# Cross-attention on one core: gamma steps, loads of the next batch and remainders of weights in another order

## What is computed

```python
a = layer_norm(ctx) * gamma + beta              # [512, 1024] of each batch
Q, K, V = x @ Wq.T, a @ Wk.T, a @ Wv.T          # 16 heads of 64
scores = where(mask, Q @ K.T * 64 ** -0.5, -inf)
out = softmax(scores) @ V                       # back to [512, 1024]
y = x + tanh(gate) * (out @ Wo.T)
```

## Time and profile before

| | us |
|---|---|
| median of 3 runs (1990.89 to 1993.92) | 1991.17 |
| profiled execution | 1995.22 |
| its span | 1993.4 |
| TensorE (PE) busy | 1941.4 (97%) |
| VectorE (DVE) busy | 1618.6 (81%) |
| GpSimd (POOL) busy | 1573.6 (79%) |
| ScalarE (ACT) busy | 1284.8 (64%) |
| DMA queue q1, share of 16 engines | 51.4% |

### The profile page before, as it was taken

How to read it: one execution, slowest core, us unless ns; L and a number is a source line. 1 busy time by engine, 2 the same in 40 slices (tenths; PEclk the granted TensorE clock), 3 DMA queues, 4 the chain that set the end, 5 groups by cost and what they waited for, 6 DMA issues and landing times.

```text
span 1993.4 us, 26143 instructions
## 1 busy us (share of the span) xinstructions
PE 1941.4 (97%) x8528; PEld 1570.1 (79%) x8528; DVE 1618.6 (81%) x2089; ACT 1284.8 (64%) x2375; POOL 1573.6 (79%) x851
## 2 busy tenths in 40 slices
PE   6999999999999999999999999999999999999997
PEld 5777778887788777888788887888778888788886
DVE  7688878887788777888788887888778888778878
ACT  5767776567656576655865668665686566756554
POOL 3899997789867888678876789768897688966664
PEclk9999999999999999999999999999999999999999
DMA  7577545664365543664446553555534655435422
GB/s 265 180 246 254 180 158 188 207 218 159 122 216 179 196 175 111 232 203 167 153 149 216 186 204 121 182 198 186 203 124 156 234 161 191 150 129 191 155 103 107
DMA packets 150039, 356.67 MB, mean 179 GB/s; under 512 B 63504, under 2 KB 67600, under 8 KB 149008
## 3 DMA queue, kind: packets, MB, share of 16 engines
q1 hardware_dynamic: 149904, 354.99, 51.4%
HBM read 303.54 MB, written 51.39 MB: 178 GB/s over the span
## 4 chain that ended last, share of the span: by engine, by line
PE 65%; ACT 8%; POOL 8%; DVE 7%; DMA 6%; issue 3%; SPq 2%; POOLq 0%; ACTq 0%; DVEq 0%
PE pj L485 12%; PE pj L487 12%; PE pj L489 12%; PE sc L438 4%; PE sc L442 4%; PE sc L439 4%; PE pv L432 4%; PE sc L412 4%; PE sc L413 4%; PE pv L433 4%; POOL a_lo L1189 4%; DVE mq L847 3%; DMA rows<-rstd 2%; POOL p_lo L1147 2%; ACT prob L657 2%
## 5 line engine op out<-in xcount | busy, mean ns | idle before, releaser
L1147 POOL TENSOR_TENSOR p_lo<-prob,p_hi 128x1024 fp32r<-128x1024 f32 x256 | 613.7, 2409 | 151.3 <-ACT p_hi L662 151.3
L485 PE MATMUL pj<-a_hi,w_hi 128*128 128x512 f32 x1024 | 403.9, 394 | 10.3 <-DVE qt L897 3.2
L489 PE MATMUL pj<-a_hi,w_lo 128*128 128x512 f32 x1024 | 401.4, 392 | 0.0
L487 PE MATMUL pj<-a_lo,w_hi 128*128 128x512 f32 x1024 | 401.1, 392 | 0.0
L847 DVE TRANSPOSE_TENSOR_REDUCE mq<-sc 128x32 f32<-128x1024 f32 x256 | 303.7, 1224 | 72.6 <-PE sc L413 71.7
L657 ACT ACTIVATE prob<-prob 128x1024 f32<-128x1024 f32 x256 | 271.6, 1061 | 101.2 <-DVE prob L869 100.8
L914 DVE SCALAR_TENSOR_TENSOR xy<-sc,tg_b,xy 128x1024 f32<-128x1024 f32 x244 | 304.7, 1272 | 15.0 <-PE sc L442 8.9
L869 DVE TENSOR_TENSOR prob<-sc,m_b 128x1024 f32<-128x1024 f32 x256 | 301.5, 1219 | 4.4
L1151 POOL TENSOR_TENSOR prob<-prob 128x1024 f32<-128x1024 f32 x126 | 302.5, 2401 | 0.0
L662 ACT CAST p_hi<-prob 128x1024 fp32r<-128x1024 f32 x256 | 269.3, 1052 | 3.5
L485 PEld LDWEIGHTS pj<-a_hi,w_hi 128*128 128x128 f32 x1024 | 193.1, 189 | 60.3 <-issue 6.1
(11 more groups left out here) (129 smaller groups left out, 3735.5 us busy)
## 6 DMA issues: line engine op xcount, KB each, us to landing
w_hi<-kept_hi SPq DMA_DIRECT2D x224, 512.0 KB, 3.7
w_lo<-kept_lo SPq DMA_DIRECT2D x224, 512.0 KB, 4.7
xy<-in_xT SPq DMA_DIRECT2D x32, 512.0 KB, 6.2
cx<-in_ctx SPq DMA_DIRECT2D x32, 512.0 KB, 8.3
kept_hi<-w_hi SPq DMA_DIRECT2D x32, 512.0 KB, 5.4
kept_lo<-w_lo SPq DMA_DIRECT2D x32, 512.0 KB, 6.1
out_y<-xy SPq DMA_DIRECT2D x7, 2048.0 KB, 9.8
cx<-in_ctxT SPq DMA_DIRECT2D x24, 512.0 KB, 7.3
```

The costliest lines, as they stand in the source:

```text
L485: pe.matmul(dst, w_hi[:, w, cols], s_hi[:, i], start=i == 0, stop=False)
L487: pe.matmul(dst, w_hi[:, w, cols], s_lo[:, i], start=False, stop=False)
L489: mm = pe.matmul(dst, w_lo[:, w, cols], s_hi[:, i], start=False, stop=i == KT - 1)
L1147: pool.tensor_tensor(p_lo[:, 2 * i:2 * i + 2], prob[:, h, 2 * i:2 * i + 2], f32(p_hi[:, 2 * i:2 * i + 2]), ALU.subtract).then_inc(pl_done, 1)
```

## The change

Five edits.

1. *Gamma steps.* In "ready" bodies (1,6) to (6,6), three of the eight `a_float` stand at the start, ahead of `gather_maxima`, four between the two `q_high`, the last behind the last `p_high`. Before, they stood in four pairs between exp and the casts. TensorE's wait for all eight at the start of a "switch" body is kept for batch 0 alone.
2. *Loads.* In `batch`, what belongs to the next batch is issued ahead of the kept weights of Q, K and O instead of behind them.
3. *spread_rows* is issued one body later than before (table SPREAD_ROWS: pair 0 in j = 3, pair 1 in j = 4), right behind `exchange_sums`. TURNED_NORM still has centre 0 in (b,3) first half; centre 3 goes from (b,5) to (b,4) second half.
4. *Remainders.* DVE forms those of six more pieces, (WQ,1), (WK,1), (WV,1), (WQ,2), (WV,2), (WQ,3), and POOL no longer does. In the first two bodies `v_high` and `v_low` stand earlier.
5. `norm_quarter` 1, in body (0,5), stands behind the subtraction of the maxima instead of ahead of the maximum over keys.

```diff
+BY_V = {(WK, 0), (WV, 0), (WQ, 1), (WK, 1), (WV, 1), (WQ, 2), (WV, 2), (WQ, 3)}
...
+SPREAD_ROWS = {3: 0, 4: 1}
 TURNED_NORM = {(3, 0): (("centre", 0), ("scale", 0)), (3, 1): (("centre", 1),), (4, 0): (("scale", 1), ("centre", 2)),
-               (4, 1): (("scale", 2),), (5, 0): (("centre", 3), ("scale", 3))}
+               (4, 1): (("scale", 2), ("centre", 3)), (5, 0): (("scale", 3),)}
...
                     exchange_sums(k - 1)
+                    if j in SPREAD_ROWS:
+                        spread_rows(b, SPREAD_ROWS[j])
+                    if j == 0:
+                        next_mask(b)
+                    for s in CTX_LOADS[1].get(j, ()):
+                        load_ctx(b, s)
+                    if j in TURNED_LOADS:
+                        load_turned(b, TURNED_LOADS[j])
+                    if 2 <= j <= 5:
+                        load_x(b, j - 2)
                     load_kept(WQ, (j + 2) % PAIRS, k)
                     load_kept(WK, (j + 2) % PAIRS, k)
...
-                    if j == 0:
-                        next_mask(b)
...
-                    if j in TURNED_LOADS:
-                        load_turned(b, TURNED_LOADS[j])
-                        spread_rows(b, TURNED_LOADS[j])
-                    if 2 <= j <= 5:
-                        load_x(b, j - 2)
...
-                    if kind == "switch" and h == 0:
+                    if kind == "switch" and h == 0 and b == 0:
                         pe.wait_ge(at_done, b * KT + 2 * KT)
...
+                if kind == "ready":
+                    for i in range(3):
+                        a_float(b, i)
...
                 gather_maxima(k, 0)
                 hand_out_maxima(k, 0)
+                if k < 2:
+                    v_high(k)
...
-                v_high(k)
+                if k >= 2:
+                    v_high(k)
...
                 q_high(k, 0)
+                if kind == "ready":
+                    for i in range(3, KT - 1):
+                        a_float(b, i)
                 q_high(k, 1)
...
                 p_high(k, 1, 1)
+                if kind == "ready":
+                    a_float(b, KT - 1)
...
+            def split_w(b, kind, pair):
+                if b > 0 or (kind, pair) not in BY_V:
+                    return
+                m = NUMBER[kind, pair]
+                dve.wait_ge(wlo_done, m)
+                dve.wait_ge(whi_done, m + 1)
+                dve.tensor_tensor(w_lo[:, kind], w_raw[:, m % 2], f32(w_hi[:, kind]), ALU.subtract).then_inc(wlo_done, 1)
...
-                if b == 0 and (j, 0) in NORM:
+                if b == 0 and j == 6:
                     norm_quarter(NORM[j, 0])
                 key_maxima(k, 0)
                 spread_maxima(k, 0)
+                if k < 2:
+                    v_low(k)
                 subtract(k, 0, 0)
                 subtract(k, 0, 1)
+                split_w(b, WV, j + 1)
+                if b == 0 and j == 5:
+                    norm_quarter(NORM[j, 0])
```

More of the change, by code:

```diff
@@ L755, in body @@
                 exp(k, 0, 0)
-                v_high(k)
+                if k >= 2:
+                    v_high(k)
                 p_high(k, 0, 0)
                 exp(k, 0, 1)
-                if kind in ("prepare", "ready"):
+                if kind == "prepare":
                     a_float(b, 0)
@@ L980, in body @@
                 spread_maxima(k, 0)
+                if k < 2:
+                    v_low(k)
                 subtract(k, 0, 0)
                 subtract(k, 0, 1)
+                split_w(b, WV, j + 1)
+                if b == 0 and j == 5:
+                    norm_quarter(NORM[j, 0])
                 if kind == "prepare":
                     accumulate(k, 0, 0, 0, 0, b % 2)
-                v_low(k)
+                if k >= 2:
+                    v_low(k)
                 if begun:
@@ L1007, in body @@
                 subtract(k, 1, 1)
+                split_w(b, WQ, j + 2)
                 if b == 0 and (j, 1) in NORM:
@@ L1130, in _ @@
             k_low(-1, 1)
+            split_w(0, WQ, 1)
             dve.wait_ge(tg_done, 1)
             mask_factor(-1, 0)
+            split_w(0, WK, 1)
             run_bodies(body, last_body)
@@ L1137, in split_w @@
             def split_w(b, kind, pair):
-                if not splits(b, kind, pair):
+                if not splits(b, kind, pair) or (kind, pair) in BY_V:
                     return
                 m = NUMBER[kind, pair]
+                ge(pool, wlo_done, m)
                 pool.wait_ge(whi_done, m + 1)
@@ L1248, in _ @@
             deviations(-1, 1)
-            pool.wait_ge(wlo_done, 3)
-            for one in FIRST_SPLITS[3:]:
-                split_w(0, *one)
             run_bodies(body, last_body)
```

11 lines of the change are left out of this document (2 added, 9 removed).

## The result

| | us |
|---|---|
| before, median of 4 runs (1988.90 to 1993.92) | 1991.03 |
| changed, median of 4 runs (2040.01 to 2042.62) | 2041.57 |
| ratio | 1.0252, interval 1.0234 to 1.0270 |
| changed, profiled execution, and its span | 2040.01, 2038.2 |

What follows compares the result with a forecast made beforehand. TensorE was taken as the bound, busy throughout a plain body of 29.70 us. The terms, -19 - 3.7 + 39 - 3.6 = +12.7, gave 2007.9 us for the profiled execution and 2004 for the median, range 1964 to 2022.

Steps and rivals of the forecast that it cites:

- Step 1: Ready and switch bodies of batches 1 to 6: moved gamma steps remove TensorE's waits, -3.2 us a batch, -19 in all.
- Step 2: Bodies (b,4): V's kept weights no longer late, as SP's exchange of rows leaves the end of (b,3); -3.7 us.
- Step 4: Body (0,5): nobody waits at once for the quarter behind the subtraction; body falls to about 30.3, -3.6 us.
- step 5: Batch 0, remainders on DVE: gain mostly given back, 0 (-3 to +3); DVE and POOL excluding each other would add some 5.
- Step 3: Bodies (b,4), (b,5): rows exchanged behind the sums come late, delaying POOL's halves and Q's weights; 6.5 us a batch, +39.
- upper bound of +68: Exchange of rows: writes need 9.9 us after the last issue, everything 2.7 later in both bodies; 11 to 12 a batch.
- First exchange: Pair 0's rows in (b,3): SP passes at about 23.3 us, TensorE in (b,4) is 5.4 us late.
- Second exchange: Pair 1's rows in (b,4): sums and exchange start 4 us later, rows back at 32.4, TensorE loses another 1.1 us.
- A: Rival: rows land quickly, writes take 1.4 to 3 us, the exchange costs 0; -26.3, 1965 us, chance 0.19.
- B: Rival: exchange bites half, SP passes near 21.5, (b,4) loses 3, (b,5) nothing; 1983 to 1991 us, chance 0.14.
- C: Rival: TensorE pauses twice and falls to the lower clock twice, or writes need 9.9; +65, 2030 us, chance 0.10.
- D: Rival: gamma gain fails, late `z_done` holds ACT at the head of (b,6); up to +19, chance within the others' ranges.

Runs made afterwards that it cites:

- e1: Changed kernel with the moved loads and the moved exchange of rows put back where the kernel before has them; 1968.33 us, ratio 0.9897 to before.
- e6: Changed kernel, but each of the four writes of rows takes 128 items of 128 bytes instead of 4 bytes; 1968.97 us.
- e4: Changed kernel with Q's kept weights ahead of the exchange of rows and POOL's turned steps half a body or more later; 2000.43 us.
- e7: Changed kernel, but each of the four writes of 4-byte items is made twice, the second into another part of DRAM; 2058.36 us.

## Why the prediction was wrong, point by point

**Step 1, gamma steps (-19): right.** (b,6) 29.7 as forecast, (b,7) 30.5 against 30.6, -19.8 in sum; alone, 21 us.

**Step 2, V's kept weights (-3.7): over-sized, and not owed to the moved loads.** With the old order on SP, (b,4) summed to 181.95, 180.88 and 180.96 without edit 1, and to 179.45 and 178.39 with it. The waits differ from execution to execution and were the largest in the one trace read. Whether the gamma steps shorten them is open; five executions don't settle it.

**Step 4, body (0,5) (-3.6), and step 5 (0).** (0,5) takes 31.30, not 30.3. Edits 4 and 5 together measured -0.7 us (-2.6 to +1.2). The 5 us that step 5 set beside its zero did not show: the eight remainders on DVE in the changed kernel take 1.22 us each (1.215 to 1.226), the six new ones no longer than the two of before. The 3.01 us of the quarter, which the prediction set beside such holding, is no case of two large inputs: its operation has one. It does stand out against 1.04 to 1.24 for the other three quarters in the same trace, and POOL subtracted beside it (`w_lo`, from 190.92 for 2.40 us); why, no run here settles. The three terms beside the exchange were forecast at -26.3 and measured -21 (1968.33 against 1989.06).

**Step 3, the exchange (+39): the mechanism was right, the size was not; this is the step that failed, forecast at +39 and measured at some +71.** 2041.57 against e1's 1968.33 is 73, and by the two ratios to before (1.0252 - 0.9897) it is 71. That is at and a little over the prediction's own upper bound of +68, the case that the writes need longer. Its parts:

- *First exchange.* SP passes 24.7 us into (b,3) on average over the six (23.75 to 27.20), not at 23.3. The prediction took the 7.3 us between the queue's going idle and the fetch; from the last issue to the last landing it is 7.6 to 9.9, with an idle queue. From there to the landing of Q's remainder it is 12.8, not 11.8. (The prediction's 9.2, from which 11.8 was made, is the row at 1118.10: that is V's remainder, not Q's, since `sums<-rq` follows it. It has x and two kept halves in it, as meant, so the figure could serve.) So Q's weights come 7.8 us into (b,4) (37.5 - 29.7), not 5.4, and the body is 8.3 late. The lower clock took its part: 3.6 us of it were forecast, but the granted share is 0.95 in only two of the six bodies, 0.91 in three and 0.87 in (2,4).
- *Second exchange*, charged at 1.1 and measured at 3.8. "The sums and the second exchange start 4 us later" was the wrong sentence. The sums of (b,4) are issued 19.1 in, on average, not 15.4. POOL's `key_sums` of (b,3) ends 16.05 into (4,4), not 14.6, and the sums follow another 1.9 behind it. SP passes at 32.1, where the forecast had 27, and Q's weights land at 41.9 instead of 36.5. TensorE, 8.3 late, wants them at 39.8 (29.7 + 8.3 + 1.8). That leaves 2.1, and the traces show 1.0 to 3.5, mean 2.0. In three of the six (b,5) the clock then falls to its lower level a second time; in the other three `p_low` comes late as well, by 0.3 to 0.6 us. "Q's weights just make it" rested on 36.5 against 36.9, a margin of 0.4 us behind a chain of six estimates.

**Rivals.** A needs a quick trip, and e6 shows just that: 1969 where A said 1965. B did not occur: SP passed at 24.7 and not near 21.5. C had two branches. The slower writes came, in part; its second pause within (b,4) did not, and instead (b,5) had a long one. In all +50 against C's +39 (2030). C's chance of 0.10 was too low: every wait in the chain delays the next, so a term that is 1.4 short at the start is 5 short at the end. D did not occur: `z_done` came in time.

## What to carry to other kernels

A queue that waits in order passes its wait on to everything behind it. Before moving such a wait, list every transfer behind it with its due time, and ask for the last as well as for the first; in e4 the one rescued load gave its place to the next. Part the exchange instead: write early, wait one body later. And when a forecast ends with a margin smaller than the spread of its terms over the instances in the trace, put the case beyond the margin into the sum: if a second wait is to hide behind the lateness of a first, ask whether the first also delays its start. Here the second exchange cost 4.8 us by itself and still 3.8 behind the first, not 1.1.

## What was not expected of the hardware

With no load under way, the last of four writes of 128 items of 4 bytes from SBUF to DRAM lands 7.6 to 9.9 us after its issue (the twelve exchanges of the changed kernel, mean 8.2), and the first of them 5.5 to 7.1 after its own. With items of 128 bytes it is 1.5, the median of 48 (e6). Eight writes instead of four leave the mean at 8.2 (e7), so the time is not per item.

Nor is it spent on moving the bytes, as far as the records tell. The DMA view of the changed kernel, 1142 to 1154 in 40 slices of 0.3 us, around the exchange of body (4,3):

```profile
DMA  2212122202100000000000000000000000000999
GB/s 24 18 13 26 11 18 2 2 0 2 1 1 0 0 0 0 0 0 0 0 0 0 0 0 0 0 0 0 0 0 0 0 0 0 0 0 0 20 24 10
```

The last packets stand in the twelfth slice, which ends at 1145.6; SP passes at 1151.92, 6.3 us later. In e6 the issues end at 1105.5 (1103.70 + 1.79) and SP passes at 1106.58. What the chip does in the 6.3 us no run here shows.
